# One core of Trainium2: the second layer norm's result written in fp8, and turned by fp8 products with an fp8 identity in place of f32 transposes

## The reference, cut to what matters

```python
t = t + _L1_attn_ref(_ln_t(t), ...)
t = t + _L1_ffn_ref(_ln_t(t), W1, b1, W2, b2)

def _qlinear(x, W, b):              # q_mul: to 5 exponent, 2 mantissa bits; q_acc: to f16
    y = q_acc(jnp.einsum('bsk,nk->bsn', q_mul(x), q_mul(W)))
    return q_acc(y + q_mul(b))
h = jax.nn.relu(_qlinear(x, W1, b1))
y = _qlinear(h, W2, b2)
```

## Time and profile before

| | |
|---|---|
| median of 3 runs | 5125.53 us (5116.55 to 5125.58) |
| the profiled execution | 5131.13 us |
| its span, first to last instruction | 5129.0 us |
| TensorE matmul busy | 4814.5 us, 94% of the span, 40842 instructions |
| TensorE weight load busy | 4288.8 us, 84% |
| VectorE busy | 3774.6 us, 74% |
| ScalarE busy | 3823.1 us, 75% |
| GpSimd busy | 2494.5 us, 49% |

### The profile page before, as it was taken

The page is one execution under the profiler, slowest core; times in us unless marked ns, Lnnn a source line. Parts: engine busy times, 40 slices in busy tenths (PEclk is TensorE's granted clock), DMA queues, the critical chain, the costliest instruction groups (busy, mean ns, idle before and its releaser), DMA issues.

```text
span 5129.0 us, 121783 instructions
## 1 busy us (share of the span) xinstructions
PE 4814.5 (94%) x40842; PEld 4288.8 (84%) x40842; DVE 3774.6 (74%) x10869; ACT 3823.1 (75%) x7819; POOL 2494.5 (49%) x2603
## 2 busy tenths in 40 slices
PE   8999994799999999999999999999999999999975
PEld 7888883588888888888888888888888888888853
DVE  3444443257888888888888888888888888888884
ACT  3444442378888888888888888888888888888852
POOL 2334432144555555555555555555555555555542
PEclk9999997699999999999999999999999999999985
DMA  6778775366666666666666666666666666666541
GB/s 204 242 226 242 245 232 139 91 164 178 171 171 175 175 176 175 175 175 172 173 175 176 175 176 174 178 175 174 174 170 173 176 174 176 173 175 175 154 113 31
DMA packets 781423, 893.15 MB, mean 174 GB/s; under 512 B 236243, under 2 KB 689292, under 8 KB 768652
## 3 DMA queue, kind: packets, MB, share of 16 engines
q1 hardware_dynamic: 780556, 885.27, 63.0%
q10 hardware_dynamic: 264, 0.10, 0.0%
HBM read 500.64 MB, written 384.61 MB: 173 GB/s over the span
## 4 chain that ended last, share of the span: by engine, by line
PE 69%; DVE 7%; ACT 3%; issue 3%; DMA 0%; POOL 0%; DVEq 0%; POOLq 0%
PE ps L1019 12%; PE ps L1044 10%; PE ps L1031 10%; PE ps L1060 6%; PE ps L1059 6%; PE ps L1071 6%; PE ps L1083 5%; PE ps L1109 5%; PE ps L1120 4%; PE ps L1096 3%; PE ps L1131 3%; ACT ps L789 1%; DVE gv L944 1%; ACT spec L784 1%; DVE mean L894 1%
## 5 line engine op out<-in xcount | busy, mean ns | idle before, releaser
L719 POOL TENSOR_SCALAR gv<-gv 96x400 f32<-96x400 f32 (+1 forms) x512 | 600.2, 1172 | 1719.5 <-DVE xn L959 1629.1
L340 PE MATMUL cps<-toep,xin 114*128 114x190 f32 (+2 forms) x3456 | 777.2, 339 | 42.4 <-issue 23.1
L836 ACT ACTIVATE y<-ps 128x1089 f16<-128x1089 f32 (+1 forms) x512 | 573.3, 1120 | 327.0 <-PE ps L1109 327.0
L1044 PE MATMUL ps<-hid,fa 121*128 121x384 f32 (+1 forms) x2048 | 731.2, 439 | 71.9 <-DVE t L983 59.6
L1019 PE MATMUL ps<-fb,acol 100*96 100x100 f32 x7936 | 772.3, 250 | 14.3 <-DVE spec L951 13.6
L1019 PEld LDWEIGHTS ps<-fb,acol 100*96 100x96 f32 x7936 | 734.4, 164 | 25.4 <-issue 25.2
L286 ACT ACTIVATE xo<-cps 128x180 f32<-128x180 f32 (+3 forms) x576 | 367.4, 638 | 450.8 <-PE cps L343 450.8
L1031 PE MATMUL ps<-w1t,xnt 97*121 97x192 f32 x3200 | 702.6, 330 | 0.7 <-ACT xnt L827 0.7
L317 DVE SCALAR_TENSOR_TENSOR xo<-cps,xo 128x180 f32<-128x180 f32 (+3 forms) x576 | 362.4, 629 | 459.3 <-ACT xo L286 458.7
L1059 PE MATMUL ps<-w2t,spec 97*100 97x96 f32 x3968 | 672.6, 251 | 4.1 <-ACT y L836 4.1
L1060 PE MATMUL ps<-w2t,spec 96*100 96x96 f32 x3968 | 675.3, 252 | 0.0
(11 more groups left out here) (104 smaller groups left out, 10640.5 us busy)
## 6 DMA issues: line engine op xcount, KB each, us to landing
a_d<-arow SPq DMA_DIRECT2D x448, 288.0 KB, 4.1
acol<-a_d SPq DMA_DIRECT2D x192, 600.0 KB
xin<-in_items SPq DMA_DIRECT2D x96, 1008.0 KB
g_d<-mixed SPq DMA_DIRECT2D x256, 300.0 KB
tok<-x_d SPq DMA_DIRECT2D x64, 1134.4 KB
out<-o_sb SPq DMA_DIRECT2D x448, 136.1 KB
x_d<-xo SPq DMA_DIRECT2D x48, 990.0 KB, 12.1
grow<-g_d SPq DMA_DIRECT2D x128, 312.0 KB, 10.8
```

The lines of the kernel that those rows point to most:

```text
L340: last = nc.tensor.matmul(ps[2 * (m % DEEP)][:, (r0 - o0) * GC:(r1 - o0) * GC], xb, toep[e % 2][0:GP, c, at * GC:(at + r1 - r0) * GC], sta ...
L719: nc.gpsimd.tensor_scalar(v, v, 0.0, None, ALU.max).then_inc(v_cut, 1)
L836: nc.scalar.activation(y16[n % 2][:, :, 0:w], ps[:, MIXP:MIXP + FM, 0:w], ACT.Copy).then_inc(y16_ready, 1)
L1044: nc.tensor.matmul(ps[0:M, ROW, 0:(s1 - s0) * H], fa[:, :], hid[part][:, 0:s1 - s0, :].rearrange("p j h -> p (j h)"), start=True, stop=Tru ...
```

## The change

The xn2 tiles become fp8 (float8e5), and normalise writes them so, with overflow going to infinity as the reference's rounding has it (saturate=False). A new fp8 tile ident8 holds the identity; VectorE casts it once from `ident` while the stage is set up. In turn2 each f32 transpose becomes an ordinary fp8 product, with the same stationary operand (the column of xn2, now fp8) and ident8 streamed past it, into the same place of PSUM in f32. ScalarE's copy behind it is unchanged; it rounds values that are already fp8.

```diff
-        xn2 = [sb(f"xn2{s}", [U, JC, C]) for s in range(2)]
+        ident8 = sb("ident8", [U, U], F8)
+        xn2 = [sb(f"xn2{s}", [U, JC, C], F8) for s in range(2)]
...
+                nc.vector.tensor_copy(ident8[:, :], ident[0:U, 0:U], saturate=False)
                 nc.vector.memset(mixed[:, PAIRS_K, :], 0.0)
...
                     last = nc.vector.tensor_scalar(xn2[n % 2][:, j - c0, :], t2[i % 2][:, j, :],
                                                    mean2[k][:, S + j:S + j + 1], rstd[k][:, S + j:S + j + 1],
-                                                   ALU.subtract, ALU.mult)
+                                                   ALU.subtract, ALU.mult, saturate=False)
...
                 for j in range(c1 - c0):
-                    last = nc.tensor.transpose(ps[0:C, TURNED, 128 * j:128 * j + U], xn2[n % 2][:, j, :],
-                                               ident[0:U, 0:U])
+                    last = nc.tensor.matmul(ps[0:C, TURNED, 128 * j:128 * j + U], xn2[n % 2][:, j, :],
+                                            ident8[:, :], start=True, stop=True)
```

## The result

The changed kernel takes 5084.98 us (median of 4 runs, 5073.81 to 5089.58) where the kernel before takes 5125.56 beside it: a ratio of 0.9917, with a 95% interval of 0.9904 to 0.9931. The profiled execution took 5083.75 us with a span of 5082.0, which is 47.4 and 47.0 less than before. Lines move by two: turn2 is now L1133, normalise L961, residual L985, the rows products L1046, columns L1021.

What follows compares the result with a forecast made beforehand. TensorE's streaming was taken to bound seven slots in eight, a ScalarE-VectorE chain the eighth. Net 0.862 us an image over 59 images is 50.9, less 0.2 for the cast: 5074.8 us against the median, range 5060 to 5102.

Steps and rivals of the forecast that it cites:

- An fp8 product, 0.053: In turn2, fp8 products come 0.053 us apart instead of 0.103, saving 0.050 each when another such product follows.
- The rival of a bound load: In turn2, the 96-column load paces products at 0.080 us; gain 27 us, total 5098; chance 0.06.
- the rival that a product does no better than a transpose: In turn2, fp8 products pace like the transposes, 0.103 us; gain nought, total 5125; chance 0.05.
- The last product saves less: At the end of turn2, columns' slow f32 load follows, so the last product saves 0.017 us, not 0.050.
- The rival of a hidden load: Columns' f32 load behind turn2 stays hidden, the last product saves 0.050 too; 62.5 us gained, 5063; chance 0.07.
- The slots: On TensorE, a slot with three columns saves 0.117 us, the one with four 0.167; eight slots 0.986 an image.
- What the eighth slot takes back: Once an image the rows product waits on VectorE's residual: 0.117 us given back, another 0.007 behind it; net 0.862.
- the chain has a fixed length: From TensorE's columns over ScalarE and VectorE to the waiting rows product, length stays constant, so 0.117 us is given back.
- the slack of slot 7: In the slot behind the waiting one, 0.11 us lies between residual and rows product, absorbing all but 0.007 of 0.117.
- ScalarE's cover: ScalarE's copies come 0.117 us later against columns; L775's wait of 0.25 us covers that, leaving 0.13.
- VectorE's write: Normalise writes fp8 at an unchanged 320 ns; 0.65 us idle ahead of L941 hides changes in seven of eight slots.
- The slower rival: Normalise's fp8 writes lengthen each instruction, losing from 0.29 us more; at 0.40 the total is 5145; chance 0.03.

Runs made afterwards that it cites:

- Product_alone: Changed kernel with normalise writing f32 again and turn2's fp8 products made from a fixed fp8 tile; 5083.97 us, ratio 0.9910 to the kernel before.
- norm_alone: Changed kernel with normalise still writing fp8, but turn2 transposing a fixed f32 tile as before; 5126.01 us, ratio 0.9994 to the kernel before.
- Half_stream: Changed kernel with only 61 of the 121 identity columns streamed in turn2, loads unchanged; 5077.59 us, ratio 0.9897 to the kernel before.
- turn_ahead: Changed kernel with turn2 issued ahead of up on TensorE, so columns follows up's long products; 5113.02 us, ratio 0.9961 to the kernel before.
- both_fixes: Changed kernel with GpSimd held once an image until the variance is through, residual ahead of variance, inverse root behind next slot's residual; 5046.14 us.
- root_later: Changed kernel with VectorE's residual ahead of the variance and the inverse root moved behind the next slot's residual; 5048.81 us, ratio 0.9848.

## Why the prediction was right, point by point

- **What bounds.** Right. The clock of the full pipeline stayed at 1.00. Product_alone shows that time taken off one TensorE group shows in the total, and norm_alone that VectorE's write does not.
- **An fp8 product, 0.053.** Right: three products in 0.16 us up to the next group, 0.053 each, and columns' second product late by 0.03, which was the second of the two pictures that the prediction gave. Half_stream shows that streaming binds and that the 96-column load would bind at some 0.043; the 0.055 was only an upper bound. The rival of a bound load (0.080) falls with it. So does the rival that a product does no better than a transpose: the rule of the Trainium skill, "Perfetto Trace Analysis", section Transposes, does not hold for this case, where the transpose of f32 is 0.103 and the fp8 product 0.053.
- **The last product saves less.** Right in size, and placed by turn_ahead: the load costs 0.03 us, seen as columns' 1.57 for 1.54, and gone when columns follows up. The rival of a hidden load is out.
- **The slots.** Six of eight to a hundredth: 7.48 and 7.69.
- **What the eighth slot takes back.** Right in kind, too small in size: 0.117 + 0.007 was counted and about 0.20 is given back (0.986 less 0.79). Two terms. First, the step that failed is "the chain has a fixed length". From L1046 to the waiting L1046 are 3019.16 - 3010.58 = 8.58 us, where the same step before was 8.53, read from 3034.56 to 3043.09. Timeline of the kernel before, where that step starts and where GpSimd's L719 stands against L941 (3037.88):

```profile
3034.56 0.52 PE L1044 MATMUL ps<-hid,fa 121*128 121x192 f32 x2
...
3037.32 1.20 POOL L719 TENSOR_SCALAR gv<-gv 96x400 f32<-96x400 f32 x1 [3.34 <-DVE xn L959]
```

  The variance stands behind GpSimd's instructions, and those come later against the gate: L721 starts 0.44 us ahead of L943, where L719 started 0.56 ahead of L941. GpSimd waits for normalise, which comes later against the slot now, as ScalarE's out_up copy and VectorE's widening behind it do. So a delay that the prediction called covered, by VectorE's idle time ahead of L941, reached the chain by way of GpSimd. Five kernels bear this out. As the lead of GpSimd's L721 over the gate shrinks, 0.56 us (before), 0.44 (after), 0.42 (half_stream), 0.31 (turn_ahead), the variance grows, 2.89, 2.95, 2.97, 3.07 us; norm_alone has the 0.56 and 2.90 of before; and from the rows product to the first variance instruction are 4.89 us in all (medians of 46 or 47 images). With GpSimd held back the variance takes 1.36 us with fp8 turns and with f32 turns, so the difference is GpSimd's. Second, the slack of slot 7 was taken as 0.11, and about 0.07 of the 0.12 was kept, so the slack was some 0.06. The row used, the start of L1044, was not the right one: the product that has waited is recorded as started some 0.05 us early against the group behind it. Timeline of the kernel after, slot 7:

```profile
3025.91 0.46 DVE L985 TENSOR_TENSOR t<-ps,t_res 121x288 f32<-121x288 f32 x1 [0.24 <-DVE rstd L912]
...
3026.52 0.56 PE L1046 MATMUL ps<-hid,fa 121*128 121x192 f32 x2
...
3026.92 0.65 PE L1033 MATMUL ps<-w1t,xnt 97*121 97x192 f32 x3
```

  From the first L1046 to the next group are 0.40 us here, as in the waiting slot of the kernel before (3043.09 to 3043.49), and 0.35 in its slot 7 (3050.56 to 3050.91). The step of 0.15 from L983 to a waiting L1044 was thus 0.05 too short, and that was read as slack.
- **ScalarE's cover.** Right: L777 waits 0.13 us for columns where L775 waited 0.25 (medians), as counted.
- **VectorE's write.** Right: 320 ns, and norm_alone's image is that of before. The idle time ahead of L941 was said to be there in seven slots of eight; the trace of before has that wait 240 times in 48 images, five slots of eight. With no cost to hide it made no difference. **The slower rival** needed 0.29 us an instruction and had nothing.
- **The sum.** The 59 images gave 45.6 us in place of 50.9; the profiled execution took 5083.75 for 5080.4. The median of the runs, 5084.98 for 5075, lies inside the range. Of these 10 us, 5 are the two terms above; the rest is within the spread of the runs, 5074 to 5090.

## What to carry to other kernels

Read a saving on a full engine slot by slot, and look in the slots that wait for what gives it back. The same edit was worth 0.54 to 0.79 us an image, by where the other engines stood, and never the 0.99 of its own sum. The wait that takes a gain back may be worth more than the gain: here GpSimd's being held back once an image, for 1.3 us that it had to spare, brought 1.1 us an image more. But look where the held-back work lands: in both_fixes it ran beside VectorE's cast, and the same hold was worth nothing. And a chain's length is not a constant while it runs beside an engine that can block it: compare the same instruction's durations in several places before calling it fixed.

## What was not expected of the hardware

- Of VectorE's variance instructions on 50 f32 elements, one takes 0.19 to 0.24 us where no GpSimd instruction is under way, and 0.49 to 0.85 where it comes under one, ending 0.05 to 0.12 us behind it. VectorE's reciprocal (L908) is not held so: it takes 0.45 us and ends 0.29 ahead of GpSimd's L727.
- VectorE's cast from f16 to fp8 (1092 elements) takes 1.26 us with a GpSimd instruction under way at its start and 0.92 without (both_fixes, root_later).
- VectorE writes fp8 from f32 as fast as f32 (320 ns for 96 elements).
- A load of 96 fp8 columns lets products follow 0.043 us apart; 16 f32 products with a load of 96 columns each are slower by 0.03 in all behind a group of fp8 products (1.57 for 1.54) and by 0.05 behind one of half the columns (1.59).
- A wait of the weight loads that the trace gives to "issue" was one for a PSUM bank that ScalarE was still reading (0.26 us).
